# Attention with two rings of PSUM banks, three and two pairs, and the score tiles issued in two groups of four row groups

## What is computed

```python
x = x + attn_a(layernorm(x))   # rotation, codebook, rms norm
x = x + ffn(layernorm(x))      # 8 experts of 256, the two best per token
# attn_b: 16 heads of 8 elements, E = 128
q = einsum('bse,hde->bhsd', x, Wq) + bq ; k, v likewise
scores = einsum('bhsd,bhtd->bhst', q, k) / sqrt(8)
w = softmax(scores, axis=-1)
o = einsum('bhst,bhtd->bhsd', w, v)
x = x + o.transpose(0, 2, 1, 3).reshape(B, S, 128) @ Wo.T + bo
x = x + ffn(layernorm(x))
```

## Time and profile before

| | us |
|---|---|
| three runs, median | 1502.6 |
| lowest, highest | 1468.61, 1514.92 |
| the profiled execution | 1479.49 |
| its span, first to last instruction | 1477.7 |
| TensorE, weight loads busy | 1343.2, 743.3 |
| VectorE, ScalarE, POOL busy | 1136.6, 932.9, 74.2 |
| mean granted clock of TensorE | 0.913 of full speed |
| first reduction of a first pass, first exponential | 329.3, 369.3 |
| last exponential | 1252.6 |

### The profile page before, as it was taken

One profiled execution on the slowest core, in us unless ns is written; L12 is line 12 of the kernel. 1 busy time (PEld: TensorE's weight loads), 2 busy tenths in 40 slices (PEclk: granted clock), 3 DMA queues, 4 the chain that ended last, 5 costly groups with the idle time before them and its releaser, 6 DMA issues.

```text
span 1477.7 us, 21707 instructions
## 1 busy us (share of the span) xinstructions
PE 1343.2 (91%) x7955; PEld 743.3 (50%) x7955; DVE 1136.6 (77%) x2645; ACT 932.9 (63%) x1746; POOL 74.2 (5%) x72
## 2 busy tenths in 40 slices
PE   2779999886999999999999999999999888999999
PEld 1468898772323333333333333324333222898898
DVE  7587787769767787898878888878888850787786
ACT  1146566451756678777768767768877766556555
POOL 1032000010000000000000000000000000000000
PEclk8789999995857899998989999989999966999999
DMA  4100000000000000000000000000000000000000
GB/s 168 32 1 1 1 1 1 1 1 0 1 1 0 1 0 1 1 1 1 1 1 1 1 1 0 1 0 1 1 1 1 1 1 1 8 8 8 16 8 16
DMA packets 6120, 10.83 MB, mean 7 GB/s; under 512 B 1907, under 2 KB 3574, under 8 KB 5878
## 3 DMA queue, kind: packets, MB, share of 16 engines
q1 hardware_dynamic: 6014, 9.45, 1.9%
HBM read 7.28 MB, written 2.10 MB: 6 GB/s over the span
## 4 chain that ended last, share of the span: by engine, by line
PE 72%; DVE 16%; ACT 8%; issue 3%; DMA 0%; SPq 0%; DVEq 0%; ACTq 0%
PE six L1203 17%; PE six L1026 15%; PE acc L1271 14%; DVE mxp L826 9%; ACT PB L504 5%; PE six L1015 4%; PE six L1017 4%; PE six L1016 4%; PE six L1131 4%; ACT tr L477 2%; PE misc L1015 1%; PE misc L1138 1%; PE misc L1144 1%; PE misc L925 1%; PE misc L1017 1%
## 5 line engine op out<-in xcount | busy, mean ns | idle before, releaser
L504 ACT ACTIVATE PB<-six 128x512 f32<-128x512 f32 x1024 | 556.0, 599 | 247.8 <-PE six L1203 236.9
L826 DVE TENSOR_REDUCE mxp<-six 128x2 f32<-128x1024 f32 x512 | 600.0, 1217 | 102.4 <-PE six L1131 101.3
L1203 PE MATMUL six<-Q,K 32*128 32x512 f32 x1024 | 360.8, 519 | 38.2 <-ACT PB L504 35.6
L1203 PEld LDWEIGHTS six<-Q,K 32*128 32x128 f32 x1024 | 147.8, 198 | 387.3 <-ACT PB L504 345.2
L1271 PE MATMUL acc<-PB,Vg 128*32 128x512 f32 x2048 | 308.6, 678 | 9.8 <-ACT PB L504 6.3
L1026 PEld LDWEIGHTS six<-w2s,PB 128*128 128x128 f32 x2048 | 247.4, 192 | 9.4
L1026 PE MATMUL six<-w2s,PB 128*128 128x128 f32 x2048 | 251.1, 276 | 0.0
L428 ACT ACTIVATE PB<-six 128x512 f32<-128x512 f32 x256 | 151.6, 599 | 144.4 <-PE six L1017 124.1
L1131 PE MATMUL six<-K,Q 32*128 32x512 f32 x1024 | 191.8, 529 | 25.2 <-DVE mxp L826 24.6
L716 DVE SCALAR_TENSOR_TENSOR x<-six,wexp,x 128x128 f32<-128x128 f32 x512 | 143.8, 343 | 49.0 <-PE six L1026 47.3
L761 DVE TENSOR_TENSOR PB<-PB 128x512 f32<-128x512 f32 x128 | 98.8, 772 | 50.8 <-ACT PB L428 48.2
(11 more groups left out here) (192 smaller groups left out, 940.3 us busy)
## 6 DMA issues: line engine op xcount, KB each, us to landing
x<-in_x SPq DMA_DIRECT2D x4, 512.0 KB, 5.7
SC<-in_w_om SPq DMA_DIRECT2D x1, 2048.0 KB, 14.2
out<-x SPq DMA_DIRECT2D x8, 256.0 KB, 2.0
VH<-in_w SPq DMA_DIRECT2D x1, 1024.0 KB, 9.5
Vg<-in_wqs SPq DMA_DIRECT2D x1, 256.0 KB, 7.6
Vg<-in_wks SPq DMA_DIRECT2D x1, 256.0 KB, 5.9
cst<-in_cst SPq DMA_DIRECT2D x1, 81.5 KB, 3.3
nwb<-in_nw SPq DMA_DIRECT2D x1, 64.0 KB
```

What stands on the lines that cost most here:

```text
L504: act.activation(PB[:, k % 2, j, :], scores, ACT.Exp).then_inc(G_("exp_done"), 1)
L826: dve.reduce_max(mxp[:, th, t, 2 * i:2 * i + 2], sm[:, i, :].rearrange("p (a n) -> p a n", a=2), AX.X).then_inc(G_("max_done"), 1)
L1203: pe.matmul(sl[:, j % banks, :], K[rows, g, t * P:(t + 1) * P], Q[rows, g, u * BLK:(u + 1) * BLK], start=True, stop=True).then_inc(G_("s2_ ...
```

## The change

Seven of the eight banks form two rings; `acc` stays apart. ScalarE reads from a ring of three banks (`ACT_BANKS`: two of `six`, and `misc`), VectorE from a ring of two pairs. A table (`bank_order`) numbers all uses of each ring in program order: exponentials and ScalarE's side tasks (`act_task`) in the one, reductions and VectorE's side tasks (`max_task`: turned maxima, turned outputs, the product with Wo) in the other. A use waits until the use three (or two) numbers earlier has been taken, and ScalarE and VectorE take them in that order.

TensorE's order in a step becomes: PV, the task for ScalarE, score tile 3 of this step and 0 of the next with the first pass of heads 1 and 2, the task for VectorE, score tiles 1 and 2 of the next step with the first pass of heads 0 and 3. The last group has three banks like the others. A task for ScalarE stands ahead of the step's last exponential, one for VectorE between the step's two reductions.

K and Q are now summed by POOL: ScalarE's second pass of a projection applies the mask (with biases made once, `mbias`), and `tr` has two halves. The prologue goes through the same loop, with the values and the projection of group 1 as its ScalarE tasks.

```diff
+def act_task(s):
+
+    G, kk = divmod(s, STEPS)
+    if G < 0:
+        return ("v", kk) if kk < 2 else ("proj", 1, kk - 2) if kk < 6 else None
+    b, g = divmod(G, NG)
+    if g == 0 and b > 0 and kk in (3, 8):
+        return "rows", b - 1, kk // 8
+    if kk in (4, 5, 6, 7) and G + 2 < GROUPS:
+        return "proj", G + 2, kk - 4
+    if g == 3 and b < B - 1 and kk in (9, 10):
+        return "v", 2 * b + 2 + kk - 9
+    if g < 2 and b < B - 1 and kk == 14:
+        return "ln", 2, 2 * b + 2 + g
+    if G == GROUPS - 1 and kk == 8:
+        return "ln", 3, 0
+    return None
+
+
+def max_task(s):
+
+    G, kk = divmod(s, STEPS)
+    if G < 0:
+        return ("turn", 0, 0) if kk == 11 else None
+    b, g = divmod(G, NG)
+    if kk == 2:
+        return "turn", G, 1
+    if kk == 11 and G + 1 < GROUPS:
+        return "turn", G + 1, 0
+    if kk == 12:
+        return "out", 2 * G
+    if g == 0 and b == 0:
+        return None
+    if kk == (3 if g else 1):
+        return "out", 2 * G - 1
+    if g == 0 and kk in (9, 10):
+        return "wo", b - 1, kk - 9
+    return None
+
+
+def bank_order():
+
+    AR, DR = {}, {}
+    for s in range(STEP0, STEP1):
+        for j in range(HG):
+            if j == HG - 1 and act_task(s):
+                AR[act_task(s)] = len(AR)
+            if s >= 0:
+                AR["exp", s, j] = len(AR)
+        for i in range(2):
+            if i == 1 and max_task(s):
+                DR[max_task(s)] = len(DR)
+            if s < STEP1 - STEPS:
+                DR["max", s, i] = len(DR)
+    return AR, DR
...
-        se = six[:, 0:2]
-        sl = six[:, 0:HG]
         sm = six[:, 2:6].rearrange("p (r a) n -> p r (a n)", a=2)
         acc = ps("acc", [P, BLK])
         misc = ps("misc", [P, BLK])
+        act_banks = (six[:, 0, :], six[:, 1, :], misc[:])
...
+            def split_out(G, task):
+
+                if G == 0:
+                    pl.wait_ge(G_("qkp_taken"), task + 1)
+                else:
+                    pl.wait_ge(*act_taken("proj", G, task))
+                dst = (Q if task % 2 else K)[:, G % NG, (task // 2) * BLK:(task // 2 + 1) * BLK]
+                pl.tensor_tensor(dst, qf[:, task % 2, :], tr[:, task % 2, :].bitcast(F32), ALU.add
+                                 ).then_inc(G_("qk_split"), 1)
...
+            def proj_out(G, task):
+
+                n = 4 * G + task
+                if n >= 2:
+                    act.wait_ge(G_("qk_split"), n - 1)
+                g, q = G % NG, task % 2
+                bias = bqs[:, g:g + 1] if q else bqk[:, NG + g:NG + g + 1]
+                low_bias = mbias[:, g:g + 1] if q else mbias[:, NG + g:NG + g + 1]
+                low_scale = mbias[:, 2 * NG:2 * NG + 1] if q else nmk
+                if G == 0:
+                    act.wait_ge(G_("qkp_done"), task + 1)
+                    bank = misc[:]
+                else:
+                    bank = taken_bank("proj", G, task)
+                act.activation(qf[:, q, :], bank, ACT.Identity, bias=bias, scale=DH ** -0.5 if q else 1.0)
+                act.activation(tr[:, q, :], bank, ACT.Identity, bias=low_bias, scale=low_scale
+                               ).then_inc(G_("act_taken" if G else "qkp_taken"), 1)
+
+            def taken_bank(*key):
+                act.wait_ge(G_("act_filled"), AR[key] + 1)
+                return act_banks[AR[key] % ACT_BANKS]
...
-                    for j in range(HG):
-                        act.wait_ge(G_("s2_done"), HG * (BSTEPS * b + k) + j + 1)
-                        if j == 0 and not (first and k < 2):
-                            act.wait_ge(G_("pv_done"), BSTEPS * b + k - 1)
-                        scores = sl[:, j, :] if last and g == NG - 1 else se[:, j % 2, :]
-                        act.activation(PB[:, k % 2, j, :], scores, ACT.Exp).then_inc(G_("exp_done"), 1)
...
+            for s in range(STEP0, STEP1):
+                if s < 0:
+                    side_task(s)
+                for j in range(HG if s >= 0 else 0):
+                    if j == HG - 1:
+                        side_task(s)
+                    scores = taken_bank("exp", s, j)
+                    if j == 0 and s >= 2:
+                        act.wait_ge(G_("pv_done"), s - 1)
+                    act.activation(PB[:, s % 2, j, :], scores, ACT.Exp).then_inc(G_("act_taken"), 1)
+                    if j == 2 and s % 8 == 0 and s:
+                        acc_out(s // 8 - 1)
...
+            def taken_slot(*key):
+                dve.wait_ge(G_("max_filled"), DR[key] + 1)
+                return sm[:, DR[key] % 2, :]
+
+            def maxima(s, i):
+
+                t, th = s % STEPS // 2, s % 2
+                dst = mxp[:, th, t, 0:HG:HG - 1] if i else mxp[:, th, t, 1:HG - 1]
+                dve.reduce_max(dst, taken_slot("max", s, i).rearrange("p (a n) -> p a n", a=2),
+                               AX.X).then_inc(G_("max_taken"), 1)
...
+                if s < STEP1 - STEPS:
+                    maxima(s, 0)
+                side_task(s)
+                if s < STEP1 - STEPS:
+                    maxima(s, 1)
+                if kk in (7, 15) and s < STEP1 - STEPS:
+                    minus_max(s, kk // 8)
...
+            def free_bank(*key):
+                n = AR[key]
+                if n >= ACT_BANKS:
+                    pe.wait_ge(G_("act_taken"), n - ACT_BANKS + 1)
+                return act_banks[n % ACT_BANKS]
+
+            def free_slot(*key):
+                n = DR[key]
+                if n >= 2:
+                    pe.wait_ge(G_("max_taken"), n - 1)
+                return sm[:, n % 2, :]
+
+            def scores(s, j):
+
+                G, kk = divmod(s, STEPS)
+                u, t = divmod(kk, TPB)
+                bank = free_bank("exp", s, j)
+                if j == 0 and t == 0:
+                    pe.wait_ge(*max_taken("turn", G, u))
+                rows = slice(RB * j, RB * (j + 1))
+                pe.matmul(bank, K[rows, G % NG, t * P:(t + 1) * P], Q[rows, G % NG, u * BLK:(u + 1) * BLK],
+                          start=True, stop=True).then_inc(G_("act_filled"), 1)
+
+            def first_pass(s, i):
+
+                G, kk = s // STEPS + 1, s % STEPS
+                t, th = divmod(kk, 2)
+                if kk == 0 and i == 0:
+                    pe.wait_ge(G_("qk_split"), 4 * G + 4)
+                slot = free_slot("max", s, i)
+                for c in range(2):
+                    j = (HG - 1) * c if i else 1 + c
+                    rows = slice(RB * j, RB * (j + 1))
+                    ins = pe.matmul(slot[:, c * BLK:(c + 1) * BLK], Q[rows, G % NG, t * P:(t + 1) * P],
+                                    K[rows, G % NG, th * BLK:(th + 1) * BLK], start=True, stop=True)
+                ins.then_inc(G_("max_filled"), 1)
...
-                    second_pass(0)
-                    second_pass(1)
-                    if not more:
-                        second_pass(2)
-                    if k > 0:
-                        times_values(b, k - 1, first)
-                    elif not first:
-                        times_values(b - 1, BSTEPS - 1)
-                    if more:
-                        second_pass(2)
-                    second_pass(3)
...
-                    if task:
-                        if prev is not None:
-                            pe.wait_ge(*prev)
-                        task[0](*task[1])
-                        prev = (G_(task[2]), task[3])
-                    if more:
-                        first_pass(2 * STEPS * (Gn + 1), (g + 1) % NG, kk, 0)
-                        first_pass(2 * STEPS * (Gn + 1), (g + 1) % NG, kk, 1)
...
+            for s in range(STEP0, STEP1):
+                if s > 0:
+                    times_values(s - 1)
+                fill_for_act(s)
+                if s >= 0:
+                    scores(s, 3)
+                if 0 <= s + 1 < STEP1:
+                    scores(s + 1, 0)
+                if s + 1 < STEP1 - STEPS:
+                    first_pass(s + 1, 0)
+                fill_for_max(s + 1)
+                if 0 <= s + 1 < STEP1:
+                    scores(s + 1, 1)
+                    scores(s + 1, 2)
+                if s + 1 < STEP1 - STEPS:
+                    first_pass(s + 1, 1)
+            times_values(STEP1 - 1)
+            pe.wait_ge(G_("max_taken"), len(DR))
```

More of the change, by code:

```diff
@@ L231, in ln_count, with ln_beside, h_turned, h_copied @@
             return NBLK * kind + n + 1
+        def ln_beside(kind, n):
+            return sum(("ln", *divmod(m, NBLK)) not in AR for m in range(ln_count(kind, n)))
+        def h_turned(kind, n):
+            if ("ln", kind, n) in AR:
+                return G_("act_filled"), AR["ln", kind, n] + 1
+            return G_("lnt_done"), ln_beside(kind, n)
+        def h_copied(kind, n):
+            if ("ln", kind, n) in AR:
+                return G_("act_taken"), AR["ln", kind, n] + 1
+            return G_("ht_ready"), ln_beside(kind, n)
+        def act_taken(*key):
```

(41 more changed lines are left out.)

478 lines of the change are left out of this document (168 added, 310 removed).

## The result

The changed kernel takes **1554.4 us** (median of four runs, 1545.49 to 1565.82); the kernel before took 1502.3 beside it. The ratio is 1.0518, with an interval of 1.0452 to 1.0585: slower by 5%. The forecast was 1500 us (1447 to 1562), no change; the time is in the range, but it is slower where no change was forecast. What came is rival B, which had a chance of 0.24 and a time of 1545 us.

What follows compares the result with a forecast made beforehand. Attention was taken as bound by a closed TensorE-ScalarE chain, 3.10 us per plain step, neither engine full. Terms +12 - 7 + 9 - 3 = +11 on 1479.5 gave 1490; forecast 1500 us, between 1490 and 1513, range 1447 to 1562.

Steps and rivals of the forecast that it cites:

- rival B: Attention: clock falls at every projection run, fourteen runs of 14 to 22 us low; slower, 1545 us; chance 0.24.
- Rival C: Attention: plain steps stay near 3.1 us because VectorE and POOL make the period; 1553 us; chance 0.04.
- -0.8: Third group of a batch in attention: forecast 51.1 us against 51.9 before.
- The sum for this stretch: Attention's terms: three batches +12 us, last batch's third group -7, last group +9.
- The sum of +11 us: Whole kernel: +12 for three batches, -7 last batch's third group, +9 last group, -3 prologue.
- the 35 us: Attention before the change: cost of five low-clock stretches, 110 us in all ahead of the last group.
- most full-clock groups had none: Argument against rival B: most full-clock attention groups before the change had no low stretch behind their projection run.
- the 217 from which B decides: Attention: total low-clock us, about 43 us extra clock cost over 1490, from which rival B decides.
- Rival A: Attention: clock stays up in the groups through denser plain steps, removing 35 us; 1455 us, faster; chance 0.26.
- The grouping itself gets no further gain: Plain steps: placing first-pass and score tiles on different row groups adds nothing, as they lie under waits already counted.
- Its extra 2.5 us: First group of a batch: layer norm's VectorE work meets less idle time beside attention, 2.5 us more.
- the prediction's switch of 0.71: Last group at low clock: each step now holds the score-to-PV switch, 0.71 us; 16 steps give 11, taken as +9.

Runs made afterwards that it cites:

- Experiment 1: Changed kernel with three more unused-result matmuls in each of the 56 projection steps, where TensorE waits for ScalarE's passes: 1506.8 us, ratio 1.0179.
- experiment 2: Changed kernel with TensorE issuing ScalarE's task ahead of PV instead of behind it: 1466.6 us, ratio 0.9789 to the kernel before.
- Experiment 3: Changed kernel with first-pass heads paired 0, 1 and 2, 3 again, so each four tiles use a row group twice: 1726.1 us, ratio 1.1647.
- experiment 7: Changed kernel with only the layer norm beside attention spread over more steps: 1529.9 us, ratio 1.0307 to the kernel before.
- experiment 5: Kernel of experiment 2 with the layer norm beside attention also spread over more steps: 1418.7 us, ratio 0.9556 to the kernel before.
- experiment 4: Changed kernel with the K and Q sums of groups 1 to 15 on VectorE again instead of POOL: 1557.2 us, ratio 1.0507.

## Why the prediction was wrong

**The steps were right.** The prediction's main prices, against the trace of the change (from one step's first exponential to the next one's, at full clock where not said):

| step | before | forecast | after |
|---|---|---|---|
| plain | about 3.10 | 2.61 | 2.62 |
| with a second-ring task | about 3.10 | 3.23 | 3.32 |
| projection | 3.72 | 4.24 | 4.38 |
| plain, low clock | 4.55 | 4.06 | 4.07 |
| group without projections | 51.8 | 44.6 | 44.8 |
| third group of a batch | 51.9 | 51.1 | 53.4 to 57.7, with low stretches |

Rival C fell with the first row. A third group with the clock up all the way is not in the trace of the change. Experiment 1 has it at 51.9, so -0.8 was 0.0: mostly the 0.14 of each projection step. From first to last exponential attention grew by 67 us, 884.0 to 951.1. Low time is priced by the table, roughly, as steps of other kinds have prices of their own: 175 us at 0.32 (4.55 against 3.10) make 56 before; 320 at 0.36 (4.07 against 2.62) make 115 after, or 109 if the 98 us of them in projection steps go at 0.30 (6.23 against 4.38). So 53 to 59 of the 67 are the clock, and 8 to 14 the steps. The sum for this stretch was +14 (12 - 7 + 9). The prologue gave 3.7 us (3 forecast): the first exponential came at 365.6 instead of 369.3.

**The step that failed is the choice between forecast and rival B.** The sum of +11 us has no term for the clock: it kept the 35 us of before, where the clock came to cost 53 to 59 us more. The argument against B was "most full-clock groups had none". That was read from projection steps of 3.72 us. Their window in the earlier trace rows has TensorE busy 14.27 of 14.80 us. The steps that I forecast were of another kind: the same work with over a microsecond of waiting in it. In the change TensorE was busy 6.46 of 8.75 us in two such steps, and the clock fell in the third. The evidence came from the state that the change removes. And it was weaker than I read it: four of the five low stretches ahead of the last group began within 4 us behind a projection run, not three, one of them (group 6) behind a run with TensorE busy 14.57 of 15.10 us. Why the clock fell behind those busy runs, and not behind others like them, stays open. My own sum had the 4.24, and said what TensorE would wait for; it should have carried the clock with it. Experiments 1 and 2 show the cause from two sides. With the idle time filled the falls go, although the step stays at 4.38. With the idle time taken away they go too, at 3.57. B's price was sound: its 14 to 22 us low for each of fourteen runs are 196 to 308, the records have 291 ahead of the last group, over the 217 from which B decides, and its 1545 stands against 1554. Part of the 291 lies behind layer norms, which B did not count (24 us in the three stretches that began at step 11).

**Rival A's thought was turned round.** The denser plain steps hold the clock, as the group without projections shows (1.00), but they cannot make up for the thin ones among them.

**"The grouping itself gets no further gain" was wrong.** It rested on the second group lying behind the same 0.43 as score 1. Experiment 3 shows that this 0.43 holds only if the four tiles are on four row groups. It becomes 0.66 otherwise, 0.22 in every plain step, and the clock goes with it.

**The layer norm.** Its extra 2.5 us were taken as VectorE's work alone. The wait it makes for TensorE also starts a low stretch, in 5 of the 5 such groups among 1 to 13 (experiments 1 and 2). Taking it away gave 24 us (experiment 7, on another chip than the change) and, with the task ahead of PV, 48 (1466.6 to 1418.7; experiments 2 and 5, on different chips).

**The last group** was forecast 9 us longer and was 1.5 us shorter (55.1 to 53.6). At the low clock its step is 4.06, as the prediction's switch of 0.71 more than 3.34 says. But the clock held for its first eight steps, at 2.60. The mechanism was right; what failed was that I took the clock of before for it. In experiment 5 nearly the same code (one task moved) was low almost from its start (63.8 us), so one profile doesn't tell what this group costs.

**POOL** was right at 0: a sum took 1274 to 1286 ns, as the earlier trace rows had it, and experiment 4 finds no difference.

## What to carry to other kernels

When a change makes some steps of a pipeline longer by waiting, ask for each kind of step how idle TensorE is in the new one. A clock that holds in today's steps is no evidence for tomorrow's. Thin steps cost twice, by their own length and by the slower steps behind them, so the place of one side task in TensorE's order (here ahead of PV, or behind it) can decide between 5% slower and some 2% faster. VectorE's small operations should not stand in one run ahead of an operation that TensorE waits for. Before a kernel with a clock of 0.87 is called bound by anything, fill an idle stretch with useless matmuls and look: if it gets faster, the clock is what to mend.

## What the runs showed of the hardware that was not expected

- Useless work made the kernel faster twice: 168 matmuls of 128x512 moved the ratio from 1.052 to 1.018, 64 tiles of 32x512 moved the last group from 63.8 to 49.2 us.
- The clock fell in stretches whose longest wait was 1.07 us (projection steps), and in others behind one wait of 2.16 us.
- A low clock has other prices in other steps: 0.36 of each low microsecond in plain steps of 2.62 us, 0.30 in projection steps, where ScalarE's time, which doesn't change (two exponentials take 1.09 us at either level, before), makes up more of the chain.
- Two tiles on one row group start 0.33 us apart, on different ones 0.01.
- Open: which pattern of short waits is thin enough. The last group, the same instructions in the change and in experiments 1, 3, 4 and 7, was low for 29, 38, 62, 46 and 46 us (39 and 56 in experiments 2 and 5, with one task moved). So what the clock does there hangs on more than the group's own steps. Busy time alone does not tell it either: before, the clock fell behind a run in which TensorE was busy 14.57 of 15.10 us, and in the change it held through the group without projections, with TensorE busy 38.15 of 44.80 us.
